# The causal mask of the row maxima: from bf16 matmuls into PSUM to a table that VectorE adds while it takes the maximum

## The chip, the cores and the metric

The kernel runs on one core of a Trainium2 chip. The metric is the device time in microseconds (us) of the whole kernel. Three runs of the kernel before took 1254.56, 1255.55 and 1260.43 us; the median is 1255.55 us.

## What is computed

```
x  = (8, 1024, 256) fp32                       # batches, tokens, channels
xn = layernorm(x)
q, k, v = split(xn @ W_attn + b_attn)          # 16 heads of 16 channels, rope on q and k
att = where(causal, q k^T / sqrt(16), -inf)
att = softmax(att);  y = att v
s = y @ W_proj + b_proj
g = silu( (silu(xn Wg^T) * (xn Wu^T)) Wd^T )   # 768 hidden channels, integer weights / 127
out = x + s * g
```

The softmax is over the keys up to the query's own position. The kernel subtracts each row's true maximum before the exponential, and the change concerns the pass that finds these maxima.

## The kernel before

**Units and slots.** A batch has 4 groups of 4 heads; a batch and a group make one unit, so there are 32 units. A unit has 9 steps (slots), a batch 36. In each half of a slot TensorE issues two scores matmuls for the exponentials (L781), one "maxima item" for a unit that comes 12 slots later (L809 and L824), then tasks of the table `TASKS` (projections, feed-forward blocks and transposes; most go through L854), and in the second half the products with the values (L845). The order is written out by hand and is the same on every engine: each engine runs its own in-order queue, and they meet at semaphores.

**The ring.** Maxima items and tasks share four PSUM banks, `ring`, in turn. TensorE may write a bank when its last reader has counted up `ring_free`; a reader starts when `ring_ready` says so. A maxima item takes two banks (one for each of the two halves `a` of the partitions of q and k, `SIDE` 0 and 64), a task takes one. TensorE can so be at most four banks ahead of the slowest reader.

**A maxima item.** `SEGMENTS` lists 18 items for a unit. A bank has 512 columns of fp32 scores, a row for each of 128 queries:
- kind A (4 items): 384 keys of one query tile and 128 keys of another; both touch the diagonal,
- kind B (2 items): 256 keys for each of two heads of one query tile; both touch the diagonal,
- kind E (4 items): 512 keys; touches the diagonal,
- kind F (8 items): 512 keys that all lie before the queries; no diagonal.

For A, B and E, TensorE adds the causal triangle to the last 128 columns of each segment: four matmuls per item (L824) with a 64-row identity `ident64` and a bf16 triangle `tri` of -3e38, accumulated onto the scores. Each covers 64 keys of one bank (all segments of the bank in one instruction); those of the two banks use the two halves of the rows of TensorE. A 64-key slice needs only the 64 rows of its own queries above the diagonal, so two slices make the triangle.

**VectorE** then takes the row maxima out of PSUM into `mx_a` (first 512 keys) or `mx_b` (the others), in `max_take` (L1218): one TENSOR_REDUCE for a bank of E and F, one that gives both heads for B, two for A. The last one of a bank frees it. Between them VectorE has its own parts of the tasks: `ga`, `g`, `parts`, `xl`, `ynT`, `yn`, layernorm statistics.

**Setup.** GpSimd (POOL) builds `ident64` and `tri` with memsets and affine selects; SyncE (SP) copies the triangle's upper half to partitions 64 to 127; TensorE waits for both before the first item.

Of the kernel before, what the change touches and what calls it, by code (L numbers as in the profile page):

```python
# [6 lines left out]
P = 128  # L7
# [4 lines left out]
CH = 512  # L12
# [5 lines left out]
SIDE = 64  # L18
# [10 lines left out]
NEG = -3.0e38  # L29
# [323 lines left out]
def build_program(nc, x, w_attn, b_attn, w_proj, b_proj, w_gate_t, w_up_t, w_down_t, rope_cos, rope_sin, out):  # L353
# [7 lines left out]
    with ExitStack() as ctx:  # L361
# [30 lines left out]
        ident64 = sb("ident64", [P, 2, P], bf16)  # L392
        tri = sb("tri", [P, 2, P], bf16)
# [101 lines left out]
        tri_in = sem("tri_in")  # L495
# [3 lines left out]
        const0 = sem("const0")  # L499
# [117 lines left out]
        def _(sp):  # L617
# [73 lines left out]
            def prologue():  # L691
# [17 lines left out]
                sp.wait_ge(const_ready, 7)  # L709
                sp.dma_start(tri[64:P, :, :], tri[0:64, :, :]).then_inc(tri_in, 16)  # L710
# [47 lines left out]
        def _(pe):  # L758
# [28 lines left out]
            def maxima(kind, i, slot, half):  # L787
# [4 lines left out]
                diag = [k0 + w == (t + 1) * P for t, k0, w, _ in found]  # L792
# [8 lines left out]
                for k, (t, k0, w, p) in enumerate(found):  # L801
                    for a in range(2):
                        if k == 0:
                            dst, ready = take(kind, i, t_ring, a)
                        else:
                            b = bank(kind, t_ring, a)
                            dst, ready = ring[:, b, :], ring_ready[b]
                        rows = slice(SIDE * a, SIDE * a + (MROW if whole else MAXROW))
                        mm = nc.tensor.matmul(dst[:, at:at + w], q_st[rows, g, p, t * P:(t + 1) * P],  # L809
                                              k_st[rows, g, p, k0:k0 + w], start=k == 0, stop=not diag[0])  # L810
                        if not diag[0]:
                            mm.then_inc(ready, 1)
                    at += w
                if diag[0]:
                    n = len(found)
                    pitch = found[-1][2]
                    for h in range(2):
                        keys = P if whole and h == 0 else 64
                        first = pitch - P + 64 * h
                        for a in range(2):  # L820
                            b = bank(kind, t_ring, a)
                            rows = slice(SIDE * a, SIDE * a + 64)
                            tail = ring[:, b, CH - n * pitch:CH].rearrange("p (s w) -> p s w", s=n)[:, :, first:first + keys]
# [151 lines left out]
            def prologue():  # L975
# [24 lines left out]
                pe.wait_ge(const_ready, 7)  # L1000
                pe.wait_ge(tri_in, 16)
# [196 lines left out]
        def _(dve):  # L1198
            def max_take(kind, i, slot, half):

                _, g, s = max_of(kind, i, slot)
                t_ring = ("MX", slot, half)
                par = g % 2
                found = SEGMENTS[s, half]
                if found[0][0] == found[-1][0]:
                    t, k0, w, _ = found[0]
                    parts_of_bank = [(t, k0, w, [p for _, _, _, p in found])]
                else:
                    parts_of_bank = [(t, k0, w, [p]) for t, k0, w, p in found]
                for a in range(2):  # L1210
                    b = bank(kind, t_ring, a)
                    wait_ready(dve, kind, i, t_ring, a)
                    at = 0
                    for t, k0, w, heads in parts_of_bank:
                        hs = slice(heads[0], heads[-1] + 1)
                        dst = mx_b[:, par, a, hs, t - 4:t - 3] if k0 else mx_a[:, par, a, hs, t:t + 1]
                        src = ring[:, b, at:at + len(heads) * w].rearrange("p (s w) -> p s w", w=w)
                        top_ = nc.vector.reduce_max(dst, src, AX.X)  # L1218
                        at += len(heads) * w
                    top_.then_inc(ring_free[b], 1)  # L1220
# [283 lines left out]
        def _(pool):  # L1504
# [72 lines left out]
            def prologue():  # L1577
# [9 lines left out]
                pool.memset(ident64[:, :, :], 0.0).then_inc(const0, 1)  # L1587
                pool.memset(tri[:, :, :], 0.0).then_inc(const0, 1)
                pool.memset(hf[0:64, 0, :], 0.0).then_inc(k_const, 1)
                pool.memset(hf[0:64, 1, :], float(np.uint32(0x78007800).view(np.float32))).then_inc(k_const, 1)  # L1590
                pool.wait_ge(const0, 6)
# [24 lines left out]
                for h in range(2):  # L1616
                    e = ident64[:, h, 64 * h:64 * h + 64]
                    for side in range(2):
                        pool.affine_select(out=e, in_=e, compare_op=ALU.not_equal, fill=1.0, base=-64 * side,
                                           pattern=[[-1, 64]], channel_multiplier=1).then_inc(const_ready, 1)  # L1620
                        if side == 0:
                            pool.wait_ge(const_ready, 2 * h + 3)
                pool.affine_select(out=tri[:, :, :], in_=tri[:, :, :], compare_op=ALU.is_ge, fill=NEG,
                                   base=0, pattern=[[0, 2], [-1, P]], channel_multiplier=1).then_inc(const_ready, 1)
# [92 lines left out]
```

## Time and profile before

| | |
|---|---|
| runs | 1254.56, 1255.55, 1260.43 us |
| span of the profiled execution | 1257.5 us, first to last instruction |
| its own time | not on the page; of the three runs only 1260.43 us is longer than the span, and leaves 2.9 us around it |
| TensorE (PE) busy | 1197.4 us, 95% |
| VectorE (DVE) busy | 1013.0 us, 81% |
| ScalarE (ACT) busy | 935.2 us, 74% |
| GpSimd (POOL) busy | 693.3 us, 55% |
| granted TensorE clock | 0.99 of full speed over the span |
| mask matmuls L824 | 1280, 85.9 us busy |
| maxima L1218 | 1408 instructions, 747.2 us busy |

"Busy" is the union of an engine's instruction records. Records of neighbours overlap at their ends: the sum of the single durations is larger than the busy time, and the distance from start to start is what an instruction costs a full engine. The layernorm statistics of a batch start at 536.2, 682.6, 828.9 and 975.3 us, so a batch takes 146.4 us in the middle of the run.

### The profile page before, as it was taken

The page shows a single profiled execution, that of the slowest core. Times are in us where ns is not written, and L with a number is a line of the kernel's source. Part 1 is how long each engine was busy: PE and PEld are TensorE (multiplying, and loading weights), DVE is VectorE, ACT ScalarE, POOL GpSimd, SP SyncE. Part 2 cuts the span into 40 slices and gives each one's busy share as a digit, 9 for nine tenths or more (in the row PEclk, how much of TensorE's full clock was granted, in tenths as well). Part 3 has the DMA queues.
Part 4 walks back from the last instruction along what each step waited for, and adds up shares of the span by engine and source line. Part 5 has one row for each costly group of instructions (what it writes and reads, how often), then busy time and mean ns, then how long its engine had stood idle before and what let it go on. Part 6 is the DMA issues. An engine that isn't in the chain of part 4 may idle for free.

```text
span 1257.5 us, 29932 instructions
## 1 busy us (share of the span) xinstructions
PE 1197.4 (95%) x11324; PEld 558.3 (44%) x11324; DVE 1013.0 (81%) x2098; ACT 935.2 (74%) x1736; POOL 693.3 (55%) x863
## 2 busy tenths in 40 slices
PE   3889999999999999999999999999999999999986
PEld 2334444545345443544445453454445444454433
DVE  6678988888888888888888888888888888878732
ACT  4447777787877878778777878778787787778774
POOL 4527544395535937177453946369371874446472
PEclk9879999999999999999999999999999999999999
DMA  6140020401222120400204011221204002120101
GB/s 170 47 136 2 2 86 19 119 19 60 53 72 74 35 88 32 119 19 27 85 31 115 20 63 48 86 66 30 91 28 119 19 27 86 39 73 29 42 2 51
DMA packets 56004, 73.23 MB, mean 58 GB/s; under 512 B 8398, under 2 KB 34452, under 8 KB 55860
## 3 DMA queue, kind: packets, MB, share of 16 engines
q1 hardware_dynamic: 55848, 71.30, 18.9%
q8 instruction: 90, 1.47, 0.5%
q14 instruction: 54, 0.44, 0.1%
q10 hardware_dynamic: 12, 0.01, 0.0%
HBM read 44.96 MB, written 25.17 MB: 56 GB/s over the span
## 4 chain that ended last, share of the span: by engine, by line
PE 74%; POOL 10%; DVE 6%; issue 4%; ACT 4%; SPq 1%; DMA 1%; POOLq 0%; DVEq 0%; ACTq 0%
PE ring L854 31%; PE acc L845 17%; PE st L781 11%; PE ring L809 8%; PE ring L927 2%; DVE mx_a L1218 2%; POOL hf L1542 2%; PE ring L824 2%; ACT pexp L1055 2%; POOL hT L1551 1%; PE ring L864 1%; POOL xn L535 1%; PE ring L963 1%; POOL pexp L1512 1%; PE ring L942 1%
## 5 line engine op out<-in xcount | busy, mean ns | idle before, releaser
L1055 ACT ACTIVATE pexp<-st 128x512 f32<-128x512 f32 x1152 | 623.8, 598 | 124.0 <-PE st L781 123.3
L1218 DVE TENSOR_REDUCE mx_a<-ring 128x1 f32<-128x512 f32 (+2 forms) x960 | 536.8, 611 | 50.9 <-PE ring L809 26.0
L1512 POOL TENSOR_SCALAR_AFFINE_SELECT pexp<-pexp 128x512 f32<-128x512 f32 x256 | 158.4, 638 | 412.9 <-ACT pexp L1055 412.9
L845 PE MATMUL acc<-pexp,v_pad 128*17 128x512 f32 (+3 forms) x3072 | 303.7, 490 | 5.8 <-POOL pexp L1512 4.5
L809 PE MATMUL ring<-k_st,q_st 56*128 56x512 f16 (+4 forms) x1536 | 231.4, 326 | 13.3 <-POOL k_st L1641 3.4
L781 PE MATMUL st<-q_st,k_st 58*128 58x512 f16 (+3 forms) x1536 | 231.9, 331 | 6.1 <-ACT pexp L1055 3.4
L1218 DVE TENSOR_REDUCE mx_b<-ring 128x1 f32<-128x384 f32 (+2 forms) x448 | 210.4, 528 | 25.5 <-PE ring L824 24.7
L781 PEld LDWEIGHTS st<-q_st,k_st 58*128 58x128 f16 x1536 | 61.3, 93 | 265.2 <-ACT pexp L1055 173.4
L1542 POOL TENSOR_TENSOR hf<-ga,ups 128x512 f32<-128x512 f32 x96 | 122.4, 1275 | 42.0 <-issue 41.5
L845 PEld LDWEIGHTS acc<-pexp,v_pad 128*17 128x17 f32 x3072 | 61.9, 96 | 129.1 <-issue 105.7
L1551 POOL TENSOR_TENSOR hT<-hf,hT 128x512 f16<-128x512 f32 x96 | 111.4, 1161 | 3.4
L809 PEld LDWEIGHTS ring<-k_st,q_st 56*128 56x128 f16 (+1 forms) x1536 | 80.3, 95 | 53.9 <-DVE mx_a L1218 7.1
L854 PE MATMUL ring<-w_dn,hT 128*128 128x256 bf16 x768 | 94.5, 273 | 1.5
L1282 DVE SCALAR_TENSOR_TENSOR ga<-th,ring 128x512 f32<-128x512 f32 x96 | 65.8, 685 | 33.4 <-ACT th L1109 28.5
L854 PE MATMUL ring<-xh,w 128*128 128x512 f16 x256 | 86.9, 391 | 1.4 <-DVE mx_a L1218 0.7
L824 PE MATMUL ring<-tri,ident 64*128 64x128 bf16 (+1 forms) x1280 | 85.9, 206 | 0.0
L854 PEld LDWEIGHTS ring<-w_dn,hT 128*128 128x128 f16 x768 | 72.9, 98 | 17.0 <-issue 2.1
L1094 ACT ACTIVATE parts<-ring,b_qk 128x512 f16<-128x512 f32 x64 | 44.0, 687 | 45.4 <-PE ring L854 44.4
L854 PE MATMUL ring<-xh,w_ga 128*128 128x512 f16 x192 | 74.2, 386 | 1.4 <-DVE mx_a L1218 1.4
L824 PEld LDWEIGHTS ring<-tri,ident 64*128 64x128 bf16 x1280 | 60.8, 94 | 30.7
L854 PE MATMUL ring<-xh,w_up 128*128 128x512 f16 x192 | 73.5, 383 | 0.0
L854 PE MATMUL ring<-xl,w_ga 128*128 128x512 f16 x192 | 73.4, 382 | 0.0
(152 smaller groups left out, 1536.2 us busy)
## 6 DMA issues: line engine op xcount, KB each, us to landing
parts_scratch<-parts SPq DMA_DIRECT2D x32, 512.0 KB, 2.8
q_st<-parts_scratch SPq DMA_DIRECT2D x186, 64.0 KB, 2.2
k_st<-parts_scratch SPq DMA_DIRECT2D x186, 64.0 KB, 2.2
xo<-in_x SPq DMA_DIRECT2D x32, 256.0 KB, 2.9
out<-xo SPq DMA_DIRECT2D x32, 256.0 KB, 2.2
xn<-in_x SPq DMA_DIRECT2D x7, 1024.0 KB, 6.1
q_st<-mT SPq DMA_DIRECT2D x126, 4.0 KB
xn<-in_x SPq DMA_DIRECT2D x2, 512.0 KB, 6.2
```

Source lines behind the costliest of these rows:

```text
L781: mm = nc.tensor.matmul(st[:, (GH * n + 2 * p + a) % NST, at:at + w], k_st[rows, g, p, kb * P:(kb + 1) * P], q_st[rows, g, p, q0:q0 + w], ...
L809: mm = nc.tensor.matmul(dst[:, at:at + w], q_st[rows, g, p, t * P:(t + 1) * P], k_st[rows, g, p, k0:k0 + w], start=k == 0, stop=not diag[0])
L824: mm = nc.tensor.matmul(tail, ident64[rows, h, :], tri[rows, 0:n, 0:keys], start=False, stop=h == 1)
L845: mm = nc.tensor.matmul(acc[32 * j:32 * j + D + 1, CH - w:CH], v_pad[:, kb, GH * g + j, :], pexp[:, GH * (m % NSET) + j, at:at + w], start ...
L854: mm = nc.tensor.matmul(dst, left, right, start=k == 0, stop=k == len(pairs) - 1)
L1055: nc.scalar.activation(pexp[:, GH * (n % NSET) + j, :], st[:, (GH * n + j) % NST, :], ACT.Exp, scale=1.0 / (QK_SCALE * np.sqrt(D))).then_i ...
L1094: nc.scalar.activation(parts[:, which, 0, c * CH:(c + 1) * CH], src, ACT.Identity, bias=bias)\
L1218: top_ = nc.vector.reduce_max(dst, src, AX.X)
L1282: nc.vector.scalar_tensor_tensor(out=ga[:, t[2] % 2, :], in0=th[:, th_buffer(kind, t), :], scalar=1.0, in1=src, op0=ALU.add, op1=ALU.mult) ...
L1512: nc.gpsimd.affine_select(out=t, in_=t, compare_op=ALU.is_ge, fill=0.0, base=0, pattern=[[0, GH], [1, P]], channel_multiplier=-1).then_inc ...
L1542: nc.gpsimd.tensor_tensor(hf[:, u, :], ga[:, u, :], ups[:, u, :], ALU.mult).then_inc(h_full, 1)
L1551: nc.gpsimd.tensor_tensor(hT[:, 1, m, :], hf[:, m % 2, :], hT[:, 0, m, :], ALU.subtract)\
```

## The change

The four mask matmuls of an item are gone, and `ident64` and the bf16 `tri` with its copy to the upper partitions too. `tri` is now an fp32 table of 128 x 512 in SBUF: zero in columns 0 to 383, the triangle of -3e38 in columns 384 to 511. For each segment that touches the diagonal VectorE issues `tensor_tensor_reduce` with op0 add and op1 max: it reads the segment of w columns from PSUM and the last w columns of the table from SBUF, writes the sum back in place into PSUM, and puts the maximum into `mx_a` or `mx_b`. Segments of a bank are no longer joined, so the two heads of kind B are two instructions. Kind F keeps its TENSOR_REDUCE. VectorE waits once for the table (`tri_ready`).

```
             maxima(...)            # TensorE
...
                         mm = nc.tensor.matmul(dst[:, at:at + w], q_st[rows, g, p, t * P:(t + 1) * P],
-                                              k_st[rows, g, p, k0:k0 + w], start=k == 0, stop=not diag[0])
-                        if not diag[0]:
+                                              k_st[rows, g, p, k0:k0 + w], start=k == 0,
+                                              stop=k == len(found) - 1)
+                        if k == len(found) - 1:
                             mm.then_inc(ready, 1)
                     at += w
-                if diag[0]:
...
-                            mm = nc.tensor.matmul(tail, ident64[rows, h, :], tri[rows, 0:n, 0:keys], start=False, stop=h == 1)
-                            if h == 1:
-                                mm.then_inc(ring_ready[b], 1)
...
             max_take(...)          # VectorE
...
+                if (kind, t_ring) == ("pro", ("MX",) + FRONT[0]):
+
+                    dve.wait_ge(tri_ready, 1)
                 for a in range(2):
                     b = bank(kind, t_ring, a)
                     wait_ready(dve, kind, i, t_ring, a)
                     at = 0
-                    for t, k0, w, heads in parts_of_bank:
-                        hs = slice(heads[0], heads[-1] + 1)
-                        dst = mx_b[:, par, a, hs, t - 4:t - 3] if k0 else mx_a[:, par, a, hs, t:t + 1]
-                        src = ring[:, b, at:at + len(heads) * w].rearrange("p (s w) -> p s w", w=w)
-                        top_ = nc.vector.reduce_max(dst, src, AX.X)
+                    for t, k0, w, p in found:
+                        dst = mx_b[:, par, a, p, t - 4:t - 3] if k0 else mx_a[:, par, a, p, t:t + 1]
+                        src = ring[:, b, at:at + w]
+                        if k0 + w == (t + 1) * P:
+                            top_ = nc.vector.tensor_tensor_reduce(
+                                out=src, in0=src, in1=tri[:, CH - w:CH], scale=1.0, scalar=NEG,
+                                op0=ALU.add, op1=ALU.max, accum_out=dst)
+                        else:
+                            top_ = nc.vector.reduce_max(dst, src, AX.X)
...
             prologue()             # GpSimd; SyncE's copy of tri and TensorE's waits for it are gone
...
-                pool.affine_select(out=tri[:, :, :], in_=tri[:, :, :], compare_op=ALU.is_ge, fill=NEG,
-                                   base=0, pattern=[[0, 2], [-1, P]], channel_multiplier=1).then_inc(const_ready, 1)
+                pool.affine_select(out=tri[:, CH - P:CH], in_=tri[:, CH - P:CH], compare_op=ALU.is_ge, fill=NEG,
+                                   base=0, pattern=[[-1, P]], channel_multiplier=1).then_inc(tri_ready, 1)
```

On VectorE, in the middle of the first batch, stood one reduction for each of two banks of kind E and two for each of two banks of kind A:

```order
L1218 TENSOR_REDUCE mx_a<-ring 128x1 [waits ring_ready0]
L1218 TENSOR_REDUCE mx_a<-ring 128x1 [waits ring_ready1]
L1218 TENSOR_REDUCE mx_b<-ring 128x1 [waits ring_ready2]
L1218 TENSOR_REDUCE mx_b<-ring 128x1
L1218 TENSOR_REDUCE mx_b<-ring 128x1 [waits ring_ready3]
L1218 TENSOR_REDUCE mx_b<-ring 128x1
```

At the same place of the changed program (`ISA ring,...` is the adding and maximising instruction, `ISA mx_a` or `ISA mx_b` the one that writes the maximum out) stand twice as many:

```order
L1198 ISA ring,mx_a<-ring,tri 128x512 [waits ring_ready0]
L1198 ISA mx_a 128x1
L1198 ISA ring,mx_a<-ring,tri 128x512 [waits ring_ready1]
L1198 ISA mx_a 128x1
L1198 ISA ring,mx_b<-ring,tri 128x384 [waits ring_ready2]
L1198 ISA mx_b 128x1
L1198 ISA ring,mx_b<-ring,tri 128x128
L1198 ISA mx_b 128x1
L1198 ISA ring,mx_b<-ring,tri 128x384 [waits ring_ready3]
L1198 ISA mx_b 128x1
L1198 ISA ring,mx_b<-ring,tri 128x128
L1198 ISA mx_b 128x1
```

On TensorE, in one slot of the same batch, the mask stood between an item's scores and what came next, a matmul with all 128 rows (L845) or the next half's scores (L781):

```order
L781 MATMUL st<-q_st,k_st 128x512 [waits exp_done] x2
L809 MATMUL ring<-k_st,q_st 128x512 [waits ring_free3]
L809 MATMUL ring<-k_st,q_st 128x512 [waits ring_free0]
L824 MATMUL ring<-tri,ident 128x64 x4
L781 MATMUL st<-q_st,k_st 128x512 [waits exp_done] x2
L809 MATMUL ring<-k_st,q_st 128x384 [waits ring_free1]
L809 MATMUL ring<-k_st,q_st 128x384 [waits ring_free2]
L809 MATMUL ring<-k_st,q_st 128x128 x2
L824 MATMUL ring<-tri,ident 128x2x64 x4
L845 MATMUL acc<-pexp,v_pad 17x256 [waits tri_done]
```

The changed program has there:

```order
L778 MATMUL st<-q_st,k_st 128x512 [waits exp_done] x2
L805 MATMUL ring<-k_st,q_st 128x512 [waits ring_free3]
L805 MATMUL ring<-k_st,q_st 128x512 [waits ring_free0]
L778 MATMUL st<-q_st,k_st 128x512 [waits exp_done] x2
L805 MATMUL ring<-k_st,q_st 128x384 [waits ring_free1]
L805 MATMUL ring<-k_st,q_st 128x384 [waits ring_free2]
L805 MATMUL ring<-k_st,q_st 128x128 x2
L829 MATMUL acc<-pexp,v_pad 17x256 [waits tri_done]
```

Nothing else has changed its place on TensorE: the scores, the semaphores they wait for and the matmuls behind them are the same.

## Rows read from the trace of the kernel before

**Rows 1.** The page: busy time of the engines, and the chain that ended last.
```profile
PE 1197.4 (95%) x11324; PEld 558.3 (44%) x11324; DVE 1013.0 (81%) x2098; ACT 935.2 (74%) x1736; POOL 693.3 (55%) x863
...
PE 74%; POOL 10%; DVE 6%; issue 4%; ACT 4%; SPq 1%; DMA 1%; POOLq 0%; DVEq 0%; ACTq 0%
```

**Rows 2.** Windows, one batch: PE, PEld, DVE, ACT, POOL busy us (instructions), PEclk, DMA, GB/s.
```profile
536.40:682.80 146.40, 145.07 (x1414) 68.35 (x1412) 123.88 (x257) 114.11 (x212) 84.93 (x104) 1.00 0.20 59
```

**Rows 3.** Timeline of TensorE: start us, us, engine, line, operation, names, shape, count.
```profile
608.02 0.38 PE L809 MATMUL ring<-k_st,q_st 56*128 56x512 f16 x2
608.24 0.22 PE L824 MATMUL ring<-tri,ident 64*128 64x64 bf16 x4
608.39 0.39 PE L854 MATMUL ring<-xh,w_up 128*128 128x512 f16 x1
...
611.64 0.38 PE L809 MATMUL ring<-k_st,q_st 56*128 56x256 f16 x4
611.86 0.28 PE L824 MATMUL ring<-tri,ident 64*128 64x128 bf16 x4
612.07 0.39 PE L854 MATMUL ring<-xh,w_ga 128*128 128x512 f16 x1
...
613.26 0.38 PE L809 MATMUL ring<-k_st,q_st 56*128 56x512 f16 x2
613.57 0.52 PE L845 MATMUL acc<-pexp,v_pad 128*17 128x384 f32 x4
```

**Rows 4.** Groups of VectorE's instructions by shape: busy us, mean ns, idle before.
```profile
L1218 DVE TENSOR_REDUCE mx_a<-ring 128x1 f32<-128x512 f32 x640 | 409.3, 683 | 42.1 <-PE ring L809 26.0 <-PE ring L824 11.6
L1218 DVE TENSOR_REDUCE mx_a<-ring 128x1 f32<-128x384 f32 x128 | 70.4, 550 | 4.4 <-PE ring L824 4.0
L1218 DVE TENSOR_REDUCE mx_b<-ring 128x2 f32<-128x512 f32 x64 | 41.0, 683 | 14.5 <-PE ring L824 14.5
L1218 DVE TENSOR_REDUCE mx_a<-ring 128x1 f32<-128x128 f32 x128 | 35.8, 279 | 0.0
L1254 DVE BATCH_NORM_AGGREGATE lnv<-ln 128x2 f32<-128x6 f32 x64 | 8.2, 166 | 5.1 <-issue 0.4
```

**Rows 5.** Timeline of VectorE, columns as in Rows 3.
```profile
26.63 0.15 DVE L1357 CUSTOM_DVE_ANT_0 expo<-expo 128x2 uint16<-128x2 uint16 x1
...
32.65 1.29 DVE L1218 TENSOR_REDUCE mx_a<-ring 128x1 f32<-128x512 f32 x2 [4.70 <-PE ring L824]
34.54 1.42 DVE L1218 TENSOR_REDUCE mx_a<-ring 128x1 f32<-128x384 f32 x4 [0.60 <-PE ring L824]
...
614.05 0.69 DVE L1282 SCALAR_TENSOR_TENSOR ga<-th,ring 128x512 f32<-128x512 f32 x1 [0.59 <-POOL hf L1542]
614.65 2.48 DVE L1218 TENSOR_REDUCE mx_a<-ring 128x1 f32<-128x512 f32 x4
```

**Rows 6.** Waits between 360 and 1110 us: total us, times, longest.
```profile
DVE parts L1273 <- ACT parts L1094: 20.2, 31, 0.8
DVE g L1290 <- ACT th L1117: 19.9, 37, 1.7
DVE mx_b L1218 <- PE ring L824: 15.4, 24, 0.9
DVE ga L1282 <- ACT th L1109: 12.0, 42, 0.5
DVE ynT L1295 <- ACT ynT L1120: 11.4, 16, 1.2
```

**Rows 7.** Windows of 4 and 5 us, columns as in Rows 2.
```profile
532.00:536.00 4.00, 3.98 (x48) 1.54 (x48) 3.93 (x9) 3.81 (x9) 0.64 (x1) 1.00 0.02 4
560.00:564.00 4.00, 3.34 (x34) 1.21 (x30) 3.89 (x10) 3.62 (x8) 3.94 (x6) 1.00 0.00 0
504.00:508.00 4.00, 4.00 (x34) 1.65 (x32) 3.93 (x10) 2.72 (x6) 0.00 (x0) 1.00 0.01 2
...
125.00:130.00 5.00, 4.33 (x59) 1.89 (x56) 5.00 (x12) 3.83 (x8) 5.00 (x7) 1.00 0.01 3
140.00:145.00 5.00, 3.75 (x35) 1.46 (x36) 4.89 (x10) 3.26 (x6) 4.01 (x4) 1.00 0.02 3
```

**Rows 8.** Timeline of GpSimd in the setup, columns as in Rows 3.
```profile
12.11 0.41 POOL L1623 TENSOR_SCALAR_AFFINE_SELECT tri<-tri 128x256 bf16<-128x256 bf16 x1
...
23.86 0.74 POOL L1633 COPY w_wide<-w 128x256 f16<-128x256 f16 x2 [11.09 <-DVE w L1391]
```

More of the change, by code:

```diff
@@ L391, in build_program @@
         ident16 = sb("ident16", [P, P], fp16)
-        ident64 = sb("ident64", [P, 2, P], bf16)
-        tri = sb("tri", [P, 2, P], bf16)
+        tri = sb("tri", [P, CH], fp32)
         parts = sb("parts", [P, 2, 2, T], fp16)
@@ L494, in build_program @@
         tri_done = sem("tri_done")
-        tri_in = sem("tri_in")
+        tri_ready = sem("tri_ready")
         pv_done = sem("pv_done")
@@ L791, in maxima @@
                 found = SEGMENTS[s, half]
-                diag = [k0 + w == (t + 1) * P for t, k0, w, _ in found]
                 if (s, half) == (0, 0) and (kind, g) != ("pro", 0):
@@ L809, in maxima @@
                         mm = nc.tensor.matmul(dst[:, at:at + w], q_st[rows, g, p, t * P:(t + 1) * P],
-                                              k_st[rows, g, p, k0:k0 + w], start=k == 0, stop=not diag[0])
-                        if not diag[0]:
+                                              k_st[rows, g, p, k0:k0 + w], start=k == 0,
+                                              stop=k == len(found) - 1)
+                        if k == len(found) - 1:
                             mm.then_inc(ready, 1)
                     at += w
-                if diag[0]:
[L815 to L823, printed above, removed]
-                            mm = nc.tensor.matmul(tail, ident64[rows, h, :], tri[rows, 0:n, 0:keys], start=False, stop=h == 1)
-                            if h == 1:
-                                mm.then_inc(ring_ready[b], 1)
             def values(i, g, n):
@@ L998, in prologue @@
                     task("pro", 0, t)
-                pe.wait_ge(const_ready, 7)
-                pe.wait_ge(tri_in, 16)
                 for t in PRO_MX:
@@ L1204, in max_take @@
                 found = SEGMENTS[s, half]
[L1205 to L1209, printed above, removed]
+                if (kind, t_ring) == ("pro", ("MX",) + FRONT[0]):
+                    dve.wait_ge(tri_ready, 1)
                 for a in range(2):
@@ L1586, in prologue @@
                 pool.memset(ident16[:, :], 0.0).then_inc(const0, 1)
-                pool.memset(ident64[:, :, :], 0.0).then_inc(const0, 1)
-                pool.memset(tri[:, :, :], 0.0).then_inc(const0, 1)
+                pool.memset(tri[:, :], 0.0).then_inc(const0, 1)
                 pool.memset(hf[0:64, 0, :], 0.0).then_inc(k_const, 1)
                 pool.memset(hf[0:64, 1, :], float(np.uint32(0x78007800).view(np.float32))).then_inc(k_const, 1)
-                pool.wait_ge(const0, 6)
+                pool.wait_ge(const0, 5)
                 for p in range(2):
@@ L1615, in prologue @@
                      [b_tmp[:, k, :] for k in range(4)], b_chain).then_inc(b_turned, 1)
[L1616 to L1622, printed above, removed]
-                pool.affine_select(out=tri[:, :, :], in_=tri[:, :, :], compare_op=ALU.is_ge, fill=NEG,
-                                   base=0, pattern=[[0, 2], [-1, P]], channel_multiplier=1).then_inc(const_ready, 1)
+                pool.affine_select(out=tri[:, CH - P:CH], in_=tri[:, CH - P:CH], compare_op=ALU.is_ge, fill=NEG,
+                                   base=0, pattern=[[-1, P]], channel_multiplier=1).then_inc(tri_ready, 1)
                 pool.memset(v_pad[:, :, 0:8, D:D + 1], 1.0).then_inc(ones_ready, 1)
```

4 lines of the change are left out of this document (1 added, 3 removed).

## The prediction, made before the changed kernel ran

> **What bounds the kernel now.** I read the page first, then windows of a batch, then the timelines of TensorE and VectorE, last the waits. TensorE is busy for 95% of the span and VectorE for 81%, and three quarters of the chain that ended last lie on TensorE [rows 1]. The mean hides the two ends of the run. In one batch of the middle (146.4 us) TensorE stands still for 1.3 us only, at full granted clock; VectorE has 123.9 us of work and 22.5 us of idle time [rows 2]. So TensorE sets the pace, and time taken from it shortens the batch until VectorE is the next wall, 15% away. The change moves work from the first to the second.
>
> **What TensorE loses.** The mask matmuls show as 85.9 us, but their records overlap their neighbours, so I read starts. In an item of kind E the scores start at 608.02, the mask at 608.24, the next full matmul at 608.39: 0.37 us from scores to next. In kind B it is 611.64 to 612.07, 0.43 us. In an item without a mask the scores start at 613.26 and the next matmul at 613.57: 0.31 us, not the 0.22 us after which a mask starts [rows 3]. So the step from a matmul with half the rows to one with all rows costs about 0.09 us, whoever stands last; the mask pays it today and the scores will pay it afterwards. What really goes is 0.43 - 0.31 = 0.12 us for B (and for A, whose masks have the same shape) and 0.37 - 0.31 = 0.06, say 0.07 us, for E. A unit has 6 items of A and B and 4 of E: 6 x 0.12 + 4 x 0.07 = 1.0 us, a batch 4.0 us. Without that correction it would be 6 x 0.21 + 4 x 0.15 = 1.9 us a unit, 7.4 us a batch; this is the upper bound. The smallest possible batch becomes 146.4 - 4.0 = 142.4 us.
>
> **What VectorE gains.** Three terms.
>
> The main instruction. An instruction with a second source from SBUF (`ga`, 512 columns) starts at 614.05 and the reduction behind it at 614.65; four reductions of 512 last 2.48 us with 0.683 for the last one, so 0.60 each [rows 4, 5]. A second source costs nothing. The only custom instruction of the trace lasts 0.15 us on two columns, as any small one [rows 5]. No row has PSUM as both source and destination for VectorE. Lower bound 0; as an upper bound I take one column per two ticks, a reading and a writing of the same bank in turn, which adds as much as the columns themselves: 404 ns for 384 columns (683 - 279 [rows 4]) is 1.05 ns a column, and a segment has 320 columns on average, so 337 ns. I take 0, since the engine reads, computes and writes as a stream in every row shown.
>
> The split of kind B. One reduction of 512 columns becomes two of 256. What an instruction costs beyond its columns: four reductions of 384, 128, 384 and 128 columns last 1.42 us with 0.279 us for the last; 1.141 us for 896 columns at 1.05 ns leaves 0.20 us for three, 0.066 us each [rows 5]. A batch has 16 banks of kind B: 16 x 0.066 = 1.1 us.
>
> The readout. Each of the 128 segments of a batch (64 of A, 32 of B, 32 of E) brings a second instruction that writes one column. Its price is what decides, and no row shows it. Lower bound: the 0.066 us that any instruction costs behind another. Next row: two BATCH_NORM_AGGREGATE in a row, 64 in 8.2 us busy, are 0.256 us a pair with 0.166 for the first, so 0.09 for the second [rows 4]. Upper bound: it has to wait until the main instruction has written everything (0.083 us later than a normal successor, since 0.683 - 0.600 is the overlap) and then lasts as long as the smallest instruction, 0.153 us in all when its own tail is covered, 0.236 when it is not. I take 0.066, the row of two neighbours without a wait, because there is no semaphore between the two: 128 x 0.066 = 8.4 us.
>
> [...]
>
> VectorE's work in a batch: 123.9 + 1.1 + 8.4 = 133.4 us; with 0.09 for the readout 136.5; with 0.153 144.6; with 0.236 155.2.
>
> **What else moves.** TensorE's and VectorE's waits for the table: `tri` is ready at 12.5 us, the first reduction starts at 32.65 us, and GpSimd then idles 11 us [rows 5, 8]. The setup is worth nothing either way, and the SyncE copy that goes was hidden too. Bank release: a bank is now freed by the readout, about 0.07 us later, and its scores are ready 0.15 to 0.2 us earlier. In the last 12 slots there are no maxima.
>
> **The sum.** VectorE cannot be full. It waits for ScalarE, which reads the same bank first, in `parts`, `g`, `ga`, `ynT`: 63.5 us in 750 us are 12.4 us a batch; the waits for masks (15.4 us) are of the kind that vanish when TensorE runs ahead [rows 6]. When VectorE lags, some of the first kind vanish too; I keep 8 us. So VectorE alone allows 133.4 + 8 = 141.4 us a batch, TensorE alone 142.4. Two engines that close to full and coupled by four banks don't reach either number: slices in which VectorE is full exist now (3.93 of 4 us, 3.89 of 4), and in some TensorE already loses 0.66 of 4 or 1.25 of 5 us [rows 7]. About six slices of 4 us in a batch are like that, each gets about 0.3 us more VectorE work: 2 us. That gives 144.4 us a batch, 2.0 less than now. 307 of the 320 items with a mask lie in the loop over batches, which is 7.7 batches: -15 us. The profiled span of 1257.5 us becomes 1242 us, the time of that run (1260.4, with 2.9 us around the span) 1245 us; from the median of 1255.6 us it is **1240 us**.
>
> **Rivals.**
> 1. *The readout waits for the main instruction's end* (slower). It reads what the last column leaves behind. Place: the 128 pairs of a batch. Price 0.153 us: VectorE needs 144.6 + 8 = 152.6 us a batch, +6.2 us, x 7.7 = +48 us: 1303 us; at 0.236 us 163.2 a batch, about 1385 us. It turns from gain to loss at 0.09 us (136.5 + 8 + 2 = 146.5). For it: the result is a running value; against it: no row in which a VectorE instruction waits for its neighbour without a semaphore. [...]
> 2. *No difference.* The readout costs 0.066 to 0.09 us, and the coupling eats the 4 us of TensorE: batch near 146.4 us, 1249 to 1262 us. For it: the full slices of [rows 7]; against it: the idle 22.5 us of VectorE.
> 3. *TensorE gets all of it.* VectorE's waits shrink as its load grows, and the batch is 142.4 us: -31 us, 1225 us.
> 4. *PSUM to PSUM is slow.* 128 x 0.337 = 43 us a batch at the upper bound; 133.4 + 43 + 8 = 184.5 us, +38 us, about 1550 us. Nothing in the trace speaks for it, nothing excludes it.
>
> A lower clock is not among them: the clock stays at 1.00 in a slice in which TensorE works 3.75 of 5 us [rows 7].
>
> **How the numbers follow.** A measurement of this kernel tells 0.5% from nothing, about 6 us. Forecast (1232 to 1248 us) 0.33; rival 3 0.12; rival 2 0.21; rival 1 with all prices above 0.09 us 0.27; rival 4 0.07. Faster 0.45, same 0.21, slower 0.34. For 8 in 10 the range starts at 1228 and goes to 1320 us, which takes in the 0.153 us readout and leaves out rival 4 and the dear end of rival 1.
>
> **What would show it.** Mains of 512 columns at 0.68 us and starts 0.60 us before their readout; readouts that start 0.066 us before the next instruction; VectorE near 133 us of work in a batch; 0.31 us from an E item's scores to the next full matmul; TensorE with about 2 us of new gaps in a batch, next to waits for `ring` banks released by VectorE. Wrong would be: a pair of main and readout that costs over 0.69 us for 512 columns, a main longer than 0.7 us, or a batch whose VectorE idles over 15 us while TensorE waits.

## The result and the profile after

The changed kernel takes 1248.78 us (median of four runs, 1248.09 to 1250.67), the kernel before beside it 1257.32 us (1254.56 to 1260.43): ratio 0.9937 [0.9912, 0.9961]. Measured again on another occasion (in the experiment on the sums into SBUF) it was 0.9956 [0.9940, 0.9972]. So it is faster by about half a per cent: 8.5 us between the medians here, 5.6 us the second time. The forecast was 15 us; the first interval reaches to 11 us, and 1248.78 us lies just above the forecast's 1232 to 1248 us.

The page, the busy time of the engines and the chain that ended last, as [rows 1]:

```profile
PE 1180.0 (95%) x10044; PEld 507.0 (41%) x10044; DVE 1062.2 (85%) x3250; ACT 934.1 (75%) x1736; POOL 692.0 (56%) x858
...
PE 61%; DVE 18%; POOL 8%; ACT 7%; issue 5%; SPq 1%; DMA 1%; POOLq 0%; DVEq 0%; ACTq 0%
```

TensorE has 1280 matmuls and 17 us of busy time less, VectorE 1152 instructions and 49 us more. VectorE's share of the last chain has tripled, TensorE still holds three fifths.

The window of one batch, to be held against [rows 2]: length, then PE, PEld, DVE, ACT, POOL busy us with instructions, PEclk, DMA share, GB/s.

```profile
529.40:674.90 145.50, 143.46 (x1254) 62.00 (x1250) 130.26 (x402) 113.95 (x212) 84.99 (x105) 1.00 0.20 60
```

The bounds of a window are rounded to 0.1 us. From the starts of the layernorm statistics, which repeat in these two kernels within 0.05 us between the second and the seventh batch, a batch went from 146.37 to 145.42 us: 0.95 us, where 2.0 were forecast. VectorE works 130.3 of them (124 before, 133.4 forecast) and still idles 15 us. TensorE idles 2.0 us instead of 1.3.

VectorE's groups of the maxima by shape (busy us, mean ns of one, idle time before), for [rows 4]:

```profile
L1202 DVE TENSOR_REDUCE mx_a<-ring 128x1 f32<-128x512 f32 x512 | 328.4, 684 | 17.1 <-PE ring L805 14.6
L1198 DVE CUSTOM_DVE_ANT_0 ring<-ring,tri 128x512 f32<-128x512 f32 x256 | 173.1, 718 | 8.6 <-PE ring L805 8.4
L1198 DVE CUSTOM_DVE_ANT_0 ring<-ring,tri 128x384 f32<-128x384 f32 x256 | 150.0, 586 | 5.3 <-PE ring L805 5.1
L1198 DVE CUSTOM_DVE_ANT_0 ring<-ring,tri 128x128 f32<-128x128 f32 x256 | 85.2, 333 | 0.0
L1198 DVE DVE_READ_ACCUMULATOR2_ANT mx_b<- 128x1 f32 x512 | 73.4, 143 | 0.0
```

VectorE's timeline (start us, us, engine, line, operation, names, shape, count), for [rows 5]:

```profile
611.10 1.28 DVE L1202 TENSOR_REDUCE mx_a<-ring 128x1 f32<-128x512 f32 x2
612.37 0.70 DVE L1198 CUSTOM_DVE_ANT_0 ring<-ring,tri 128x512 f32<-128x512 f32 x1
612.99 0.14 DVE L1198 DVE_READ_ACCUMULATOR2_ANT mx_a<- 128x1 f32 x1
612.99 0.73 DVE L1198 CUSTOM_DVE_ANT_0 ring<-ring,tri 128x512 f32<-128x512 f32 x1
613.64 0.14 DVE L1198 DVE_READ_ACCUMULATOR2_ANT mx_a<- 128x1 f32 x1
```

Read the starts, not the durations: the readout shows 0.14 us, but the next main starts with it, at 612.99. A pair of 512 columns moves its engine on by 0.62 us behind a reduction and by 0.65 us (612.99 to 613.64) behind another readout; a reduction takes 0.60. So a pair behind another pair costs 0.05 us more than a reduction, not the 0.153 us estimated for a readout that is waited for. Over the whole trace the median is 0.648 us for a pair of 512 columns right behind another pair, but 0.607 right behind an ordinary instruction, where a reduction takes 0.598.

TensorE's timeline, for [rows 3]. Each couple of rows is an item's scores and what follows: kind E or F with and without a wait, then kind B without and with one.

```profile
600.56 0.38 PE L805 MATMUL ring<-k_st,q_st 56*128 56x512 f16 x2
601.02 0.39 PE L838 MATMUL ring<-xh,w_up 128*128 128x512 f16 x1
...
611.96 0.38 PE L805 MATMUL ring<-k_st,q_st 56*128 56x512 f16 x2
612.27 0.39 PE L838 MATMUL ring<-xh,w_up 128*128 128x512 f16 x1
...
604.39 0.38 PE L805 MATMUL ring<-k_st,q_st 56*128 56x256 f16 x4
604.71 0.39 PE L838 MATMUL ring<-xh,w_ga 128*128 128x512 f16 x1
...
607.43 0.38 PE L805 MATMUL ring<-k_st,q_st 56*128 56x256 f16 x4
607.94 0.39 PE L838 MATMUL ring<-xh,w 128*128 128x512 f16 x1
```

The unhindered step is 0.31 to 0.32 us, as forecast. Beside it now stand steps of 0.46 and 0.51 us: the mask has gone and a wait has come. The waits of the weight loads between 360 and 1110 us (total us, times, longest) name who is waited for:

```profile
PEld st L778 <- ACT pexp L1037: 106.2, 191, 0.9
...
PEld ring L838 <- DVE mx_a L1202: 14.3, 37, 0.5
PEld ring L838 <- DVE mx_a L1198: 8.8, 21, 0.5
...
PEld ring L805 <- DVE mx_b L1198: 7.7, 26, 0.7
```

In the same stretch of the kernel before, the same view:

```profile
PEld st L781 <- ACT pexp L1055: 109.3, 190, 0.9
...
PEld ring L854 <- DVE mx_a L1218: 6.0, 21, 0.4
...
PEld ring L809 <- DVE yn L1305: 2.4, 5, 0.5
```

A load overlaps the matmul before it in these traces (in the changed kernel loads and matmuls are busy for 507.0 and 1180.0 us in a span of 1246.7), so these totals are not lost time; but between two kernels they show where waiting grew. The matmul of a task that follows an item (L854, now L838) stands for a bank that VectorE is still reading.

### The profile page after: what moved, and what is told of

Its sections match the earlier page's. It is cut to its first block, busy times and chain, and to the rows that moved or that the text cites. A ratio compares the mean times of both kernels' runs of the same rounds, so it can differ in the third digit from the quotient of the medians.

```text
span 1246.7 us, 28514 instructions
## 1 busy us (share of the span) xinstructions
PE 1180.0 (95%) x10044; PEld 507.0 (41%) x10044; DVE 1062.2 (85%) x3250; ACT 934.1 (75%) x1736; POOL 692.0 (56%) x858
## 4 chain that ended last, share of the span: by engine, by line
PE 61%; DVE 18%; POOL 8%; ACT 7%; issue 5%; SPq 1%; DMA 1%; POOLq 0%; DVEq 0%; ACTq 0%
PE ring L838 28%; PE acc L829 13%; PE st L778 9%; PE ring L805 6%; DVE ring L1198 5%; DVE mx_a L1202 4%; ACT pexp L1037 2%; PE ring L911 2%; POOL hf L1526 2%; DVE ln L1233 1%; DVE ga L1266 1%; PE ring L947 1%; POOL hT L1535 1%; ACT yT L1044 1%; DVE ynT L1279 1%
## 5 line engine op out<-in xcount | busy, mean ns | idle before, releaser
L1198 DVE CUSTOM_DVE_ANT_0 ring<-ring,tri 128x512 f32<-128x512 f32 (+3 forms) x1024 | 470.3, 523 | 29.3 <-PE ring L805 28.9
L1202 DVE TENSOR_REDUCE mx_a<-ring 128x1 f32<-128x512 f32 x512 | 328.4, 684 | 17.1 <-PE ring L805 14.6
L805 PE MATMUL ring<-k_st,q_st 56*128 56x512 f16 (+4 forms) x1536 | 243.9, 326 | 14.9 <-POOL k_st L1617 3.7
L778 PE MATMUL st<-q_st,k_st 58*128 58x512 f16 (+3 forms) x1536 | 234.4, 331 | 6.3 <-ACT pexp L1037 3.8
L805 PEld LDWEIGHTS ring<-k_st,q_st 56*128 56x128 f16 (+1 forms) x1536 | 84.9, 95 | 64.7 <-DVE mx_b L1198 12.8
L838 PE MATMUL ring<-w_dn,hT 128*128 128x256 bf16 x768 | 94.5, 273 | 2.8 <-DVE mx_a L1202 2.7
L838 PE MATMUL ring<-xh,w 128*128 128x512 f16 x256 | 85.1, 384 | 3.5 <-DVE mx_a L1198 1.7
L838 PEld LDWEIGHTS ring<-w_dn,hT 128*128 128x128 f16 x768 | 72.4, 98 | 23.7 <-issue 6.9
L838 PE MATMUL ring<-xh,w_ga 128*128 128x512 f16 x192 | 74.1, 386 | 2.1 <-DVE mx_a L1202 1.2
L838 PE MATMUL ring<-xh,w_up 128*128 128x512 f16 x192 | 73.5, 383 | 1.2
L1198 DVE DVE_READ_ACCUMULATOR2_ANT mx_b<- 128x1 f32 x512 | 73.4, 143 | 0.0
L838 PE MATMUL ring<-xl,w_ga 128*128 128x512 f16 x192 | 73.3, 382 | 0.0
L1198 DVE DVE_READ_ACCUMULATOR2_ANT mx_a<- 128x1 f32 x512 | 73.2, 143 | 0.0
```

The lines of the kernel that those rows point to most:

```text
L778: mm = nc.tensor.matmul(st[:, (GH * n + 2 * p + a) % NST, at:at + w], k_st[rows, g, p, kb * P:(kb + 1) * P], q_st[rows, g, p, q0:q0 + w], ...
L838: mm = nc.tensor.matmul(dst, left, right, start=k == 0, stop=k == len(pairs) - 1)
L1198: top_ = nc.vector.tensor_tensor_reduce(out=src, in0=src, in1=tri[:, CH - w:CH], scale=1.0, scalar=NEG, op0=ALU.add, op1=ALU.max, accum_ou ...
```

## The accounts of a batch

The starts of the trace give a batch as a sum of intervals. Call a step the time from the start of an item's scores to the start of the next block on TensorE. Over four batches, the shortest step, in which nothing is waited for, fell from 426 to 313 ns in kind A, 427 to 314 in B and 371 to 310 in E, and stayed at 310 in F. With 16 items A, 8 B and 16 E a batch: 16 x 0.113 + 8 x 0.113 + 16 x 0.061 = 3.7 us of TensorE's work are gone (4.0 forecast). The batch gained 0.95 us. All the rest of the batch, everything that is not such a step, is the same before and after within 0.1 us (117.7 and 117.8 us). So 2.75 us came back as longer steps behind items, and the question for the runs is why: because VectorE has 6.3 us more to do, or because work taken from TensorE meets something that was there all the time.

The excess of the steps over the shortest ones has two parts. One lies where a ring bank must be free: between the scores of an item's first and second bank, and ahead of the first matmul of a task. The other lies ahead of the products with the values, which take no ring bank. In us a batch, over the same four batches (a few items are left out for missing records):

| kernel | waits for ring banks | waits ahead of products |
|---|---|---|
| kernel before | 1.2 | 1.1 |
| changed | 4.5 | 0.6 |
| no masks, no table | 3.0 | 1.6 |
| masks and a table of zeros | 2.4 | 0.3 |
| no masks, half reductions | 0.7 | 1.8 |
| no masks, half exponentials | 1.7 | 1.8 |
| sums to SBUF | 3.5 | 1.1 |

In the change the waits for ring banks grow by 3.3 us, and the other part shrinks by 0.5. One case in the trace of the change: the scores of an item's first bank start at 532.56 us and those of its second at 533.15, while VectorE works off the four pairs of a B item from 531.48 to about 533. The kernels of the other rows, and of the next table, are those of the experiments below.

| kernel | median us (runs) | ratio to before [95%] | batch us | VectorE busy in it |
|---|---|---|---|---|
| before | 1257.32 (4) | | 146.37 | 123.9 |
| changed | 1248.78 (4) | 0.9937 [0.9912, 0.9961] | 145.42 | 130.2 |
| no masks, no table | 1245.16 (4) | 0.9902 [0.9873, 0.9931] | 144.93 | 123.7 |
| masks and a table of zeros | 1261.68 (10) | 1.0040 [1.0024, 1.0056] | 146.82 | 130.5 |
| kind B keeps its masks | 1253.68 (10) | 0.9974 [0.9954, 0.9994] | 145.84 | 128.1 |
| table in the first fill only | 1257.38 (10) | 0.9999 [0.9978, 1.0019] | 146.3 to 146.6 | 123.9 |
| no masks, half reductions | 1229.10 (4) | 0.9757 [0.9721, 0.9793] | 142.93 | 87.4 |
| no masks, half exponentials | 1230.66 (4) | 0.9782 [0.9753, 0.9812] | 143.78 | 123.6 |
| sums to SBUF | 1245.34 (6) | 0.9910 [0.9891, 0.9930] | 144.92 | 126.0 |
| five ring banks, two for scores | 1276.80 (4) | 1.0144 [1.0112, 1.0175] | 149.34 | 130.9 |
| changed, again | 1251.30 (7) | 0.9956 [0.9940, 0.9972] | 145.41 | 130.1 |

Each ratio is to the kernel before as it ran beside that experiment (medians of 1256.05 to 1260.24 us), so it is not the quotient of two times of this table. The batch time separates these kernels far better than the time of a run does: runs of one kernel differ by some 7 us, batches mostly by 0.05 (with B's masks, with the table in the first fill and with half exponentials by 0.3).

## The experiments

### The two halves of the change, each alone

TensorE's half: the kernel before without its masks and with its old reductions.

```
-                if diag[0]:
-                    ...   # the four mask matmuls
-                                              start=k == 0, stop=not diag[0])
+                                              start=k == 0, stop=k == len(found) - 1)
```

> The kernel before with the mask matmuls left out and nothing in their place (the maxima are taken over unmasked scores). VectorE's instructions are those of before, so only TensorE's side of the change is left. Theory C (VectorE's added work causes the new waits of TensorE): all of the 3.7 us a batch that the mask costs on TensorE comes back, batch 142.7 to 143.0 us, and with the setup's 4 us the kernel takes about 1225 us (ratio 0.975). Rival D (bank release was already just in time, so time taken from TensorE turns into waiting whatever VectorE costs): batch about 145.4 us and 1247 to 1250 us, as the changed kernel.

Measured: ratio 0.9902 [0.9873, 0.9931], a batch of 144.93 us, 1.44 less than before. Theory C fails by 2 us; rival D comes nearer but is missed by 0.5 us. The window of a batch:

```profile
526.50:671.50 145.00, 142.61 (x1256) 61.78 (x1248) 123.67 (x258) 114.01 (x213) 84.97 (x104) 1.00 0.19 60
```

VectorE does what it always did (123.67 us) and yet 3.7 - 1.44 = 2.3 us of the removed work turn into waiting, 1.8 of them at ring banks (3.0 where 1.2 stood). The waits of the weight loads between 360 and 1110 us in this kernel:

```profile
PEld st L781 <- ACT pexp L1042: 107.4, 196, 0.9
...
PEld ring L841 <- DVE mx_a L1205: 16.6, 43, 0.5
```

VectorE's half: masks kept, and the new instruction with a table of zeros beside them.

```
+                            top_ = nc.vector.tensor_tensor_reduce(
+                                out=src, in0=src, in1=table[:, CH - w:CH], scale=1.0, scalar=NEG,
+                                op0=ALU.add, op1=ALU.max, accum_out=dst)
...
+                pool.memset(table[:, :], 0.0).then_inc(tri_ready, 1)
```

> The kernel before with its mask matmuls kept, and VectorE taking the diagonal maxima by tensor_tensor_reduce with a table of zeros: only VectorE's side of the change. Theory C: VectorE gets 6.3 us more work a batch (pairs of 0.65 us for 512 columns where a reduction takes 0.60), TensorE waits 2 to 3 us more a batch in the steps from a maxima item to the next task; batch 148.5 to 149.5 us, the kernel 15 to 25 us slower than before. Rival D: the added work goes into VectorE's idle 22 us a batch, batch within 0.3 us of 146.4, kernel the same.

Measured: ratio 1.0040 [1.0024, 1.0056], a batch of 146.82 us, 0.45 more than before. That is far from theory C (148.5 to 149.5) and just outside the 0.3 us of rival D. Its window:

```profile
537.40:684.20 146.80, 145.93 (x1412) 68.82 (x1408) 130.49 (x402) 114.17 (x212) 85.07 (x104) 1.00 0.19 59
```

The halves add up: -1.44 + 0.45 = -0.99 us a batch, the change is -0.95. Over the 7.67 batches' worth of items in the loop (307 of 320, 40 a batch) that is -11.0 + 3.5 = -7.5 us. VectorE's 6.6 us of new work cost 0.45 us; the greater part of the missing gain is in the other half.

### Kind B keeps its masks

Kind B costs an extra instruction, since its joined reduction is split. Here it keeps masks and joined reduction.

```
+def by_table(kind, s, half):
+    ...
+    return diag and (not two_heads)
```

> The changed kernel, but kind B (two heads of one query tile) keeps its mask matmuls and its joined reduction; A and E go by the table. Theory C: TensorE gives up 0.9 us of its 3.7 a batch, VectorE is spared 2.7 of its 6.3 us; per us given up on TensorE, VectorE is spared three, so the batch is 0 to 0.8 us shorter than in the changed kernel (144.7 to 145.5), 1242 to 1249 us. Rival D: the batch is unchanged at 145.4 us, since waiting takes what TensorE gains or loses.

Measured: ratio 0.9974 [0.9954, 0.9994], a batch of 145.84 us (145.75 to 146.08), so 0.42 longer than in the change, and both expectations are missed. VectorE has 2.1 us less to do in a batch than in the change, TensorE keeps 8 x 0.113 = 0.9 us. So 0.9 us of TensorE's work outweigh 2.1 us of VectorE's, and taking the masks of B away is worth its split.

### The table in the first fill only

The profile of the change reaches its first batch (first layernorm statistics) at 95.0 us, that of before at 99.2. Is that the work of the change?

```
+    return diag and (kind == "pro")
```

> The table is used in the setup part (the 24 maxima items before the loop over batches) alone; the loop keeps masks and reductions. It asks whether the 4 us that the changed kernel is ahead when the first batch's layernorm starts belong to the change. If they do (mask matmuls gone from the setup, the loads of q and k issued earlier, a higher granted clock at 50 to 55 us): about 4 us faster than before, 1251 to 1254 us, with a batch of 146.4 us. If they are chance of one execution (clock between setup and loop): the same as before within 1 us.

Measured: ratio 0.9999 [0.9978, 1.0019], batch 146.3 to 146.6 us. Its profile reaches the first batch at 92.9 us, 2 us sooner than that of the change, and its runs are no faster than before. Windows of the first 60 us, first of this kernel:

```profile
0.00:60.00 60.00, 32.51 (x171) 15.31 (x172) 43.59 (x141) 26.77 (x46) 29.74 (x57) 1.00 0.40 117
```

Of the kernel before:

```profile
0.00:60.00 60.00, 34.35 (x184) 15.82 (x186) 38.09 (x101) 26.30 (x46) 25.65 (x53) 0.91 0.36 101
```

Of the changed kernel when it ran again, where it reached its first batch at 97.0 us:

```profile
0.00:60.00 60.00, 34.50 (x160) 14.89 (x160) 39.73 (x130) 26.84 (x46) 25.64 (x49) 0.91 0.38 106
```

The granted clock and the DMA rate of the setup differ from execution to execution, with one and the same kernel too: the changed kernel had a clock of 0.94 and 0.91 and a DMA rate of 111 and 106 GB/s in the first 60 us and reached its first batch at 95.0 and 97.0 us, the kernel with its sums in SBUF (below) had 0.94 and 1.00 and reached it at 94.8 and 92.4 us. So most of the 4 us can be put down to the execution that was profiled, and the times of this kernel show no gain within 0.2%. Of the 10.8 us between the two spans (1257.5 and 1246.7) 4.2 lie before the first batch's layernorm and 6.6 behind it.

### Whose reads are late: half reductions, half exponentials

Both kernels go on from the one without masks. In the first each reduction reads the first half of its columns only.

```
-                        src = ring[:, b, at:at + len(heads) * w].rearrange("p (s w) -> p s w", w=w)
+                        src = ring[:, b, at:at + len(heads) * w].rearrange("p (s w) -> p s w", w=w)[:, :, 0:w // 2]
```

> Without masks as the first experiment, and every reduction reads only the first half of each segment's columns (the maxima leave out half of the keys). A batch of that kernel took 144.93 us where the TensorE work removed (3.7 us) asked for 142.7. Theory E (TensorE waits because VectorE hands the ring's banks back too late, 1.2 us after an item's scores, although VectorE is idle for a seventh of the batch): with reads half as long the waits go, batch 142.5 to 143.2 us, kernel 1226 to 1232 us. Theory F (the waits left are those for score banks that ScalarE's exponentials hold): batch stays above 144.4 us, kernel 1241 to 1245 us.

Measured: ratio 0.9757 [0.9721, 0.9793], a batch of 142.93 us. The window and the waits of the weight loads:

```profile
518.10:661.10 143.00, 141.61 (x1256) 61.15 (x1248) 87.36 (x258) 114.01 (x213) 84.97 (x104) 1.00 0.20 61
```

```profile
PEld st L781 <- ACT pexp L1042: 107.8, 194, 0.9
...
PEld ring L841 <- DVE mx_a L1205: 8.0, 32, 0.4
```

As theory E expected, the batch comes to within 0.3 us of the 142.7 us that the kernel before would take without its 3.7 us of mask work, and the waits for ring banks fall from 3.0 to 0.7 us a batch. That is less than the 1.2 us of the kernel before, so not all of the 2.0 us gained is waiting that the removal had brought. The likely reading is that what counts is when a read ends, with TensorE four banks ahead at most, since VectorE idled 21 us a batch in the kernel without masks. But half reads take 36 us of work a batch from VectorE too (123.7 to 87.4), and no run keeps that work and shortens the release alone.

In the second the exponential covers the first 256 of 512 columns.

```
-                    nc.scalar.activation(pexp[:, GH * (n % NSET) + j, :], st[:, (GH * n + j) % NST, :], ACT.Exp,
+                    nc.scalar.activation(pexp[:, GH * (n % NSET) + j, 0:CH // 2], st[:, (GH * n + j) % NST, 0:CH // 2], ACT.Exp,
```

> Without masks as the first experiment, and every exponential computes only the first 256 of its 512 columns (the other half of the probabilities is a constant; the output is not the reference's). ScalarE gets 144 x 0.27 = 38 us less work a batch, VectorE's stays. Theory F (score banks held by ScalarE): batch falls from 144.93 to 142.7 to 143.5 us, kernel 1227 to 1233 us. Theory E (ring banks held by VectorE): batch stays within 0.4 us of 144.9, kernel 1242 to 1245 us. Both partly: 143.5 to 144.5.

The edit also sets the other half to 1 in the setup and lets GpSimd's selects keep it there. Measured: ratio 0.9782 [0.9753, 0.9812], a batch of 143.78 us (143.6 to 143.9), 1.15 less than without masks alone, the case "both partly". ScalarE's work fell by 29.5 us a batch, not 38. Window and waits:

```profile
522.40:666.00 143.60, 141.48 (x1252) 61.20 (x1248) 123.58 (x258) 84.53 (x212) 84.90 (x105) 1.00 0.19 60
```

```profile
PEld st L781 <- ACT pexp L1042: 104.9, 174, 0.9
...
PEld ring L841 <- DVE mx_a L1205: 13.1, 41, 0.5
```

So VectorE is not alone: a lighter ScalarE gives back about half of the 2.3 us. It does not do so at the score banks, as theory F had it: the waits for them hardly change (107.4 to 104.9 us), and those for ring banks fall from 3.0 to 1.7 us a batch. ScalarE reads many ring banks itself, some ahead of VectorE (`parts`, `ga`, `g`), so it can hold them up either way; the runs do not tell the two ways apart. The two shares, 2.0 us for VectorE and 1.15 for ScalarE, exceed 2.3 together; they are links of one chain and no sum. How much of the chain starts at either is left open.

### The sums into SBUF

Is it the write into PSUM that makes a pair dearer than a reduction?

```
+        sums = sb("sums", [P, 10, CH], fp32)
...
+                            turn_of[0] += 1
-                                out=src, in0=src, in1=tri[:, CH - w:CH], scale=1.0, scalar=NEG,
+                                out=sums[:, turn_of[0] % 10, 0:w], in0=src, in1=tri[:, CH - w:CH], scale=1.0, scalar=NEG,
```

> The changed kernel, but tensor_tensor_reduce writes its sums to ten scratch tiles in SBUF instead of back into the PSUM bank. In the changed kernel the main instruction of 512 columns starts its readout 0.62 us after its own start behind an ordinary instruction, 0.65 us behind another pair; a reduction takes 0.60. If the 0.02 is the write into PSUM: 0.60 and 0.63 here, VectorE's busy time 2.5 us a batch lower. If it belongs to the instruction with its accumulator: unchanged 0.62 and 0.65. The kernel's time is the changed kernel's within 0.3% either way.

Measured in this single run: 1244.36 us, batch 144.93. The groups and the timeline of VectorE:

```profile
L1201 DVE CUSTOM_DVE_ANT_0 sums<-ring,tri 128x512 f32<-128x512 f32 x256 | 165.9, 686 | 9.8 <-PE ring L807 8.9
L1201 DVE DVE_READ_ACCUMULATOR2_ANT mx_a<- 128x1 f32 x512 | 42.6, 83 | 0.0
```

```profile
599.46 0.69 DVE L1201 CUSTOM_DVE_ANT_0 sums<-ring,tri 128x512 f32<-128x512 f32 x1
600.07 0.08 DVE L1201 DVE_READ_ACCUMULATOR2_ANT mx_b<- 128x1 f32 x1
600.07 0.69 DVE L1201 CUSTOM_DVE_ANT_0 sums<-ring,tri 128x512 f32<-128x512 f32 x1
600.68 0.09 DVE L1201 DVE_READ_ACCUMULATOR2_ANT mx_b<- 128x1 f32 x1
600.68 1.28 DVE L1205 TENSOR_REDUCE mx_a<-ring 128x1 f32<-128x512 f32 x2
```

A pair now takes 0.61 us (600.07 to 600.68) instead of 0.65, the main lasts 686 ns like a reduction, and the readout 83 instead of 143. Of the 0.05 us that such a pair cost, 0.04 were the PSUM destination. It costs that only where a pair follows a pair: right behind an ordinary instruction a pair of 512 columns has a median of 0.607 us with either destination, and after a pause 0.617. VectorE's work falls to 126.1 us a batch, by 4.1 instead of the expected 2.5.

The same kernel, run more often:

> The changed kernel with its sums written to SBUF scratch tiles, timed. One look gave a batch of 144.93 us, as without any mask at all, and pairs of 0.61 us. The loop then is 1.43 us a batch shorter than before and 0.49 us shorter than the changed kernel, x 7.7: 11.0 us below the kernel before and 3.8 us below the changed one, 1244 to 1246 us if before is at 1256 (ratio to before 0.991). If the one look was chance of the setup: the same time as the changed kernel, ratio to before 0.994.

Measured: 1245.34 us (1242.39 to 1246.50), ratio 0.9910 [0.9891, 0.9930]; batch 144.92 us. That is the batch of the kernel with no masks at all: the 0.45 us of VectorE's half are gone, although VectorE still has 2.3 us more to do than there (126.0 against 123.7). The changed kernel, run beside it:

> The changed kernel once more, on the same chip as the run above, so that the two can be compared: batch 145.42 us, ratio to before 0.993 to 0.995, 1248 to 1250 us. The layernorm statistics of the first batch start anywhere between 92 and 99 us, as in the executions seen so far, which is what separates executions of one kernel by up to 7 us.

Measured: 1251.30 us (1248.98 to 1253.13), ratio 0.9956 [0.9940, 0.9972]; batch 145.41 us. The version with its sums in SBUF is 6 us (0.5%) faster, more than the 0.3% first expected, and beats both kernels.

### One more bank for the ring

If four banks are too few, five should help. The kernel holds eight banks of PSUM (three `st`, four `ring`, one `acc`); their number stays, and one goes from the scores of the exponentials (`st`) to the ring, and with it one small transpose of the setup.

```
-NST, NRING, NSET = 3, 4, 3
+NST, NRING, NSET = 2, 5, 3
```

> The changed kernel with five banks in the ring and two for the scores of the exponentials (four and three before). Theory E: the waits for ring banks (about 40 us in 750) nearly vanish; what the kernel loses at the score banks decides the sum: with two banks TensorE waits for each exponential, so I expect the ring part to win back 2.5 us a batch and the score part to cost 5 to 15 us a batch, 1270 to 1350 us. Theory F expects the loss at the score banks alone, 20 us more than that. The number of waits by releaser in the trace, not the time, tells the theories apart.

Measured: 1276.80 us, ratio 1.0144 [1.0112, 1.0175], a batch of 149.34 us, 3.9 more than the change; theory E had 1270 to 1350 us. Window and waits:

```profile
535.60:684.90 149.30, 148.00 (x1256) 64.71 (x1248) 130.94 (x401) 114.26 (x213) 84.94 (x104) 1.00 0.19 58
```

```profile
PEld st L778 <- ACT pexp L1037: 137.8, 278, 1.0
```

The waits for ring banks are nearly gone (the largest left is 2.5 us, where the change had 14.3), but the waits for score banks grew from 106.2 to 137.8 us. That fits the mechanism of the ring but does not prove it: a TensorE that is held up at the score banks also comes later to the ring, and one run cannot separate the two. The trade is a loss: here the third score bank is worth more than the fifth ring bank.

## Why the prediction was partly right, and where it failed

**What bounds the kernel.** Right: TensorE still sets the batch, with 15 us of idle VectorE beside it. Shortening TensorE alone gave time (first experiment), loading VectorE alone took little.

**TensorE's removal.** Right in mechanism: the step behind the scores is 0.31 us, and the 0.09 us from a matmul with half the rows to one with all rows (0.31 us where a half-row mask started after 0.22) are paid by the scores now. Measured 3.7 us a batch instead of 4.0: 0.061 us in E where 0.07 stood, and 0.113 in A and B instead of 0.12. Without the correction for the step it would have been 7.4 us, and by the masks' busy time 85.9 / 8 = 10.7.

**VectorE's additions.** The pair was put at 0.066 us over a reduction. It is 0.05 behind another pair (0.648 against 0.598 us), of which 0.01 remain with the sums in SBUF and 0.04 are the destination in PSUM, and 0.01 behind an ordinary instruction (0.607). VectorE gained 6.3 us a batch instead of 9.5, and works 130.2 instead of 133.4. That the estimate came this near is luck: the readout was taken as the cost and the PSUM write as free.

**The coupling: the step that failed.** It said that slices with a full VectorE would each take 0.3 us more of VectorE work, six a batch, 2 us in all. Measured: 2.75 us, which with the 0.3 us too many in the removal halves the gain, from 2.0 to 0.95 us a batch. And its cause was misplaced. The runs show 2.3 us of waiting with VectorE's work unchanged and only 0.45 us from its new work. That the term of 2 us was near 2.75 is luck too. The forecast priced what VectorE gains, and priced at nothing that TensorE arrives earlier: each of the 3.7 us brings it sooner to a ring bank that its readers, VectorE and partly ScalarE, free too late to make use of it (waits for ring banks went from 1.2 to 4.5 us a batch). How much of this is the length of single reads and how much their total work stays open. Rows of before showed such waits already (6.0 us for `ring` banks behind `mx_a`), and losses of TensorE in slices with a full VectorE [rows 7].

**The sum.** 3.7 - 2.75 = 0.95 us a batch, times 7.67 is 7.3 us: 1255.6 - 7.3 = 1248.3 us from the median that the forecast started at, 1250.0 from the 1257.32 of the runs beside the change; 1248.78 was measured, and 5.6 us of gain the second time. The setup was rightly put at nothing, as far as runs that tell 0.2% can show it.

**The rivals.** The readout that waits for its main instruction: no, the next main starts together with the readout (both at 612.99 us). PSUM to PSUM slow: there is a price, but 0.04 us a pair (0.648 against 0.611) and not 0.337. TensorE gets all of it: no; it needs reads of half the length (142.93 us). No difference, with a batch near 146.4 us: it named the right term, but the coupling takes 2.75 us of 3.7 and not all. The truth lies between this rival and the forecast.

**The signs.** Two of the three signs of being wrong came true: the mains of 512 columns last 0.718 us on average, over 0.7, and VectorE idles 15.2 us of the batch while TensorE waits, over 15. The third did not: a pair costs 0.65 us at most in the median, under 0.69.

## What to carry to other kernels

When work is taken from an engine that is 99% busy in steady state, do not assume that its saving arrives in full because the engine behind it idles 15% on average: here, with a ring of four buffers, 1.44 us of 3.7 arrived, and what counted is likely to be when each buffer is handed back (reads of half the length took another 2.0 us off the batch). Try the removal alone first, and shorten each reader in turn to see who hands back late. Where an instruction must write a result that nobody reads, try letting it write to SBUF and not to PSUM (6 us here), and compare variants by the period of a repeating stage: here it told 0.1 us in 146, while whole runs scatter by 7 us.

## What the runs showed of the hardware

- The adding and maximising instruction of 512 columns with its readout, right behind another such pair: 0.648 us from start to start with its output in PSUM, 0.611 in SBUF (medians). Right behind an ordinary instruction it is 0.607 with both; a plain reduction takes 0.598 there. The record of the main is 718 and 686 ns, that of the readout 143 and 83 ns, and the next main starts within 1 ns of the readout in both cases (776 of the 790 mains that come next after one, with either destination).
- The second instruction of the pair is nearly free: with the sums in SBUF the pair as a whole costs 0.01 us more than a reduction (0.611 against 0.598).
- Behind half-row scores a matmul with all rows starts 0.31 us after them, one with half the rows 0.22 us: 0.09 us more. That the step costs the same behind masks is worked out (an E item lost 0.061 us with its masks, not 0.15), not read from a row.
- The granted clock in the first 60 us differs between executions of one kernel: 0.94 and 0.91 in the changed one, 0.94 and 1.00 in the one with its sums in SBUF (DMA 111 and 106, 111 and 117 GB/s). The first batch started at 95.0 and 97.0, 94.8 and 92.4 us. In the middle of the run it was 1.00 in every window shown.
